# DLRM tower with a three-layer CIN: twelve instead of eleven split groups, another group order, and paced loads for the first chunk

## What is computed

```
e = stack(tbl_f[ids[:, f]] for f in 0..38)        # 512 x 39 x 16
x0 = xk = e
for W, b in ((w0,b0), (w1,b1), (w2,b2)):          # W: 39 x K x 128; K = 39, 64, 64
    z = relu(einsum('bhd,bkd,hks->bsd', x0, xk, W) + b)
    xk, direct part = z[:, :64], z[:, 64:]        # the last layer: all 128 go to direct
logit = sum over d of all direct parts            # 512 x 256
h = relu([logit, dense_ctx] @ W_top1 + b_top1)
h = relu(h @ W_top2 + b_top2)
y = h @ W_top3
```

## Time and profile before

| | us |
|---|---|
| median of 3 runs | 639.19 |
| the runs | 638.8 to 640.38 |
| the profiled execution, its own time | 637.96 |
| its span in the trace | 636.2 |
| PE busy | 604.5 (95%) |
| DVE busy | 552.8 (87%) |
| POOL busy | 459.3 (72%) |
| ACT busy | 304.1 (48%) |

### The profile page before, as it was taken

How to read it: one execution, slowest core, us unless ns; L and a number is a source line. 1 busy time by engine, 2 the same in 40 slices (tenths; PEclk the granted TensorE clock), 3 DMA queues, 4 the chain that set the end, 5 groups by cost and what they waited for, 6 DMA issues and landing times.

```text
span 636.2 us, 7265 instructions
## 1 busy us (share of the span) xinstructions
PE 604.5 (95%) x1934; PEld 364.5 (57%) x1934; DVE 552.8 (87%) x513; ACT 304.1 (48%) x375; POOL 459.3 (72%) x294
## 2 busy tenths in 40 slices
PE   0788899999999999999999999999999999999998
PEld 0334465666666565666666565656666665656653
DVE  1674999999999999999999999999999999999670
ACT  2131654535454555536454645445454646545333
POOL 6638387887878787878878787878878787728350
PEclk9899899999999999999999999999999999999999
DMA  7789887886949495877949495967859494952000
GB/s 254 163 188 222 178 196 163 183 177 143 217 102 217 92 224 119 198 154 160 205 107 218 102 217 112 213 133 180 185 128 220 93 220 99 213 124 79 2 0 0
DMA packets 28703, 98.59 MB, mean 155 GB/s; under 512 B 8113, under 2 KB 17073, under 8 KB 20498
## 3 DMA queue, kind: packets, MB, share of 16 engines
q1 hardware_dynamic: 21832, 93.81, 66.9%
q0 software_dynamic: 5120, 1.32, 2.0%
q10 hardware_dynamic: 1738, 3.33, 1.4%
HBM read 94.60 MB, written 3.84 MB: 155 GB/s over the span
## 4 chain that ended last, share of the span: by engine, by line
PE 89%; DMA 4%; POOL 3%; SPq 2%; issue 1%; ACT 1%; DVE 1%; ACTq 0%
PE z L631 41%; PE z L637 12%; PE z L639 12%; PE z L642 12%; PE z L621 4%; DMA x_rep<-x_rows 3%; POOL gathered L415 3%; PE z L625 2%; PE z L624 2%; PE d_products L718 1%; SPq L319 1%; DMA gathered<-in_tables,rows_sb 1%; PE z L692 1%; SPq L311 0%; DMA base_sb<-in_base 0%
## 5 line engine op out<-in xcount | busy, mean ns | idle before, releaser
L357 POOL TENSOR_TENSOR low<-products,high 128x1024 fp32r<-128x1024 f32 x128 | 303.9, 2389 | 112.4 <-ACT high L759 102.1
L472 DVE TENSOR_TENSOR products<-x_rep,xk 128x1024 f32<-128x1024 f32 (+1 forms) x258 | 333.5, 1339 | 22.3 <-ACT xk L743 13.3
L631 PE MATMUL z<-products,w_whole 128*128 128x512 f32 x640 | 297.8, 596 | 0.1
L759 ACT ACTIVATE high<-products 128x1024 fp32r<-128x1024 f32 x128 | 135.1, 1056 | 133.6 <-DVE products L472 125.1
L637 PE MATMUL z<-high,w_high 128*128 128x512 f32 x352 | 183.7, 522 | 3.1 <-ACT high L759 3.1
L415 POOL DMA_INDIRECT gathered<-in_tables,rows_sb x160 | 153.9, 962 | 44.3 <-issue 41.6
L631 PEld LDWEIGHTS z<-products,w_whole 128*128 128x128 f32 x640 | 121.6, 190 | 104.5 <-issue 93.3
L639 PE MATMUL z<-high,w_low 128*128 128x512 f32 x352 | 138.9, 395 | 0.0
L642 PE MATMUL z<-low,w_high 128*128 128x512 f32 x352 | 109.9, 394 | 1.6 <-POOL low L357 1.3
L637 PEld LDWEIGHTS z<-high,w_high 128*128 128x128 f32 x352 | 66.4, 189 | 41.4 <-issue 25.1
L639 PEld LDWEIGHTS z<-high,w_low 128*128 128x128 f32 x352 | 66.4, 189 | 37.2 <-issue 26.6
(11 more groups left out here) (54 smaller groups left out, 176.2 us busy)
## 6 DMA issues: line engine op xcount, KB each, us to landing
x_rep<-x_rows SPq DMA_DIRECT2D x60, 768.0 KB, 18.8
x_rep<-x_rows SPq DMA_DIRECT2D x64, 512.0 KB, 6.5
x_rows<-gathered SPq DMA_DIRECT2D x16, 225.0 KB
x_rep<-in_w ACTq DMA_DIRECT2D x2, 1280.0 KB, 9.8
gathered<-in_tables,rows_sb POOLq DMA_INDIRECT x160
x_rep<-x_rows SPq DMA_DIRECT2D x4, 384.0 KB, 11.0
x_rep<-x_rows SPq DMA_DIRECT2D x5, 256.0 KB, 6.0
x_same<-x_rows SPq DMA_DIRECT2D x15, 78.0 KB
```

Source lines behind the costliest of these rows:

```text
L357: ops.tensor_tensor(low[0:p, slot, 0:n, :], product(index, p, n), high[0:p, slot, 0:n, :].bitcast(fp32), ALU.subtract).then_inc(low_by[kin ...
L472: nc.vector.tensor_tensor(slots, rep, row.unsqueeze(1).broadcast_to([p, n, N]), ALU.mult).then_inc(made, 1 + pair)
L631: mm = nc.tensor.matmul(out, w_whole[0:p, at, i, :], product(index, p, n)[:, i, :], start=(first and i == 0), stop=(last and i == n - 1))
L759: nc.scalar.activation(high[0:p, slot, 0:n, :], product(index, p, n), ACT.Copy).then_inc(rounded, 1)
```

## The change

- `KINDS`: layer 1 from `wpwpwppwdh` to `wppwdppwdh` (group 2 becomes `p`, 3 becomes `w`, 4 becomes `d`: one split group more), layer 0 from `wsdw` to `sdww`, layer 2 from `wwpwpdpwph` to `wwppwpwpdh` (its `d` is now group 22).
- `LOW_LAG` 2 in place of 1; `GATHERS` two at group 0 and eight at group 14; `logits2` after group 6; ScalarE's `after_layer1` and `after_layer0` one group later.
- First chunk: ten parts of two tiles, and SyncE issues a part only when the part two before it has landed; the second chunk's `write_x0` stands ahead of part 7. `keep_busy(5)` in place of 3 ahead of the selection matmuls; the selector lies in ring slot 7; tile 6 is selected first.

```diff
-FIRST_PARTS = [(4, 6), (0, 4), (6, 8), (8, 10), (10, 14), (14, 17), (17, T1)]
-SELECTED = [0, 1, 6, 2, 3]
+FIRST_PARTS = [(4, 6), (0, 2), (2, 4), *((t, t + 2) for t in range(6, T1, 2))]
+SELECTED = [6, 0, 1, 2, 3]
...
-KINDS = {1: "wpwpwppwdh", 0: "wsdw", 2: "wwpwpdpwph"}
+KINDS = {1: "wppwdppwdh", 0: "sdww", 2: "wwppwpwpdh"}
...
 PAIRED = [0,2]
...
-GATHERS = {1: 1, 6: 9}
+GATHERS = {0: 2, 14: 8}
 assert sum(GATHERS.values()) == GB
-LOW_LAG = 1
-SEL_SLOT = 0
+LOW_LAG = 2
+SEL_SLOT = 7
...
         WRITES = 2
-        WRITTEN_AFTER = 2
+        IN_FLIGHT = 2
+        WRITTEN_WITH = 7
...
             for q in range(1, len(FIRST_PARTS)):
+                if q > IN_FLIGHT:
+                    sp.wait_ge(first_loaded[q - IN_FLIGHT], 32)
+                if q == WRITTEN_WITH:
+                    write_x0(sp, 1)
                 for e in range(2):
                     load_replicated(sp, 0, e, FIRST_PARTS[q], first_loaded[q])
-                if q == WRITTEN_AFTER:
-                    write_x0(sp, 1)
...
-                    if index == 8 and not (isinstance(c, int) and c == 0):
+                    if index == 6 and not (isinstance(c, int) and c == 0):
                         logits2(c - 1)
...
-            keep_busy(3)
+            keep_busy(5)
...
-                    if index == N1 + 3:
+                    if index == N1 + 4:
                         after_layer1(c)
-                    if index == N1 + N0 + 3 and not last:
+                    if index == N1 + N0 + 4 and not last:
                         after_layer0(c)
```

## The result

The changed kernel takes **712.27 us** (median of 4 runs, 710.32 to 712.84), the kernel before in the same session 639.00 us: a ratio of 1.1144, 95% interval 1.1117 to 1.1171. The forecast was 712.0 us. The profiled execution took 710.32 us, the lowest of the four, with a span of 708.5 us against 636.2.

What follows compares the result with a forecast made beforehand. TensorE's matmuls were taken to bound each chunk, with VectorE at 95%. 637.96 + 62.3 + 2.05 + 3.5 = 705.8 us, 707.0 as a median, plus 5 us for the clock gave 712 us; range 688 to 735.

Steps and rivals of the forecast that it cites:

- 1, one split group more: Each chunk: TensorE's own work falls by 0.35 us to 35.13 us; VectorE gets one low part more, GpSimd nothing.
- 2, group 22: Its low part stands behind a double product waiting for TensorE's group 20; TensorE loses 1.7 us a chunk.
- 3, group 2: Its product waits for TensorE's group 23; TensorE waits 2.3 us a chunk, 2.4 with the slower restart.
- 4, VectorE late at group 11: VectorE's low part of group 11 comes late; TensorE waits 0.7 us a chunk, between nothing and 1.2.
- 5, the chunk: A chunk takes 39.9 us for 35.48, 62.3 us over 14 chunks; the last chunk's layer 1 adds 2.05 us.
- 6, the first chunk: New loads gain 1.5 us until tile 6 lands, the new order costs 5.0 behind it: 3.5 us more.
- The clock: Group 2's new waits make the granted clock fall in one chunk in five: 3 x 1.7 = 5 us.
- the two cases seen: Clock in the old trace: half after waits of 2.73 us, or 1.52 and another; full after 1.27 us.
- The rival of unconditional falls: The clock falls in every chunk: 732.5 us; chance 0.12.
- the one with the wait of group 2 alone: Only group 2's wait stays, VectorE being in time at groups 22 and 11: chunk 37.5 us, 672 us; chance 0.10.
- The faster one: The second double product is released early, so the waits at groups 22, 2 and 11 are hidden: 632.4 us; chance 0.04.

Runs made afterwards that it cites:

- e4: The changed kernel with the ring's four empty places spread among the groups instead of all at the chunk's end; 636.98 us, ratio 0.9972.
- g1: f4 with groups 17 and 18 swapped in layer 2 (17 a `w`, 18 a `p`); 632.57 us, ratio 0.9916.
- f4: e4 with layer 0 (`wsdw`) and the selection in the order of the kernel before; 636.11 us, ratio 0.9938.
- e3: The changed kernel with `LOW_LAG` 1 in place of 2; 688.21 us, ratio 1.0760.
- e1: The changed kernel with groups 2 and 3 multiplied one by one instead of in a double product; 685.22 us, ratio 1.0728.
- f2: The kernel before with only the change's new loads of the first chunk; 634.59 us, ratio 0.9931.
- f1: The changed kernel with five extra matmuls put in group 2's wait, between `high` and `low`; 700.98 us, ratio 1.0953.
- g3: The kernel before with three ring places left empty among the groups; 639.34 us, ratio 1.0002.

## Why the prediction was right

Total, direction and mechanism held. Several terms did not, and their errors cancel.

- **1, one split group more:** held. e4 and g1, free of ring waits, take 35.37 and 35.28 us for 35.13. Most of the rest is a low part of GpSimd's that is only just in time (0.23 in f4 at group 17, 0.10 in g1 at group 19, whose pair takes 255.27 - 254.71 = 0.56; in e4 0.10 at group 17, and the other half is VectorE's at group 11). The step "GpSimd keeps its eight low parts, so nothing there" overlooked it: their number is the same, but in layer 2 two of them now stand side by side (16 and 17, in g1 18 and 19).
- **2, group 22:** 1.7 us predicted, 1.66 measured. The idle time of VectorE behind group 20 is 3.5 us; I had said 2.5.
- **3, group 2:** 2.4 us predicted, 2.39 measured, in the two pieces named (`high` 0.66, `low` 1.50; predicted 0.7 and 1.6). e3 and e1 show it to hang on group 23 and on the pair.
- **4, VectorE late at group 11:** 0.7 predicted, 0.46 measured. The low part is there at 225.92, 18.8 us after 207.10, where the sum said 19.2; TensorE would have been there at 18.5, as predicted. e1 shows that its size hangs on the wait of group 2.
- **5, the chunk:** 39.9 predicted, 39.62 measured: 62.3 us predicted for 14 chunks, 58.0 measured. This was 4 us too much. The last chunk's 2.05 us agree with the 2.0 left of the tail's 3.7 when the clock's share is taken off.
- **6, the first chunk:** the term that failed, +3.5 predicted, +0.3 measured. "I take 1.5 us as the net gain": f2 measures it alone as 4.3 us (59.30 for 63.56). The bound that the prediction took, 2.5 us for the dry stretch of the DMA engines, was too low. In the changed kernel, the DMA share from 32 to 35 us is 1.02 instead of 0.15, and the moment came at 59.62, beyond that bound. What else the new loads saved, and whether the pacing or the later write did it, was not taken apart. The second half, what the new order costs behind that moment, was predicted as 29.3 - 24.3 = 5.0 us and is (88.21 - 59.62) - (87.88 - 63.56) = 4.3.

```profile
32.00:35.00 3.00, 1.67 (x6) 0.92 (x6) 1.46 (x2) 0.00 (x0) 1.42 (x2) 1.00 1.02 222
59.62 0.68 DVE L475 TENSOR_TENSOR products<-x_rep,x_bank 64x512 f32<-64x512 f32 x1 [8.03 <-issue]
```

- **The clock:** 5 us predicted, 3 falls at 1.7 us; there were seven in the loop, 10.2 us of time with them, and one in the tail, 1.7. The kernel before has no fall in the tail, and the prediction had no term for one. That the new waits lie between the two cases seen was right; "I take one chunk in five" is what failed, it was one in two, with 1.35 to 1.8 us for each. The Trainium skill (TensorE: Matmul & The Clock Gate, "A second HAM failure mode: psum-queue depth-cycling") says that frequent small idle gaps make the clock oscillate. The trace agrees in part: the clock fell in 7 of 14 chunks with equal gaps, and not in every one. f1 shows that the gap of 1.34 us at group 2 was needed for it; gaps of about that length that stand alone (e1) made no fall in the loop.
- **Sum:** predicted 62.3 + 2.05 + 3.5 + 5 = 72.9 us of span, measured 58.0 + 2.0 + 0.3 + 11.9 = 72.2, for spans that differ by 72.3. Terms 4 to 6 were 7.5 us too large and the clock 6.9 too small. The hit within 0.3 us of the median owes as much to that luck as to the two waits, which were right to 0.1 us; the profiled run that these terms are taken from is besides 2 us under the median, where the prediction allowed 1.2.

The rival of unconditional falls, 732.5 us, and the one with the wait of group 2 alone, 672 us, didn't come. The faster one needed the second pair to be released early. e4 releases both pairs early by the ring's map, and there all the waits in the loop vanish. That the second alone would do, as the rival had it, isn't shown: in e1 the product of group 2 is released early, and group 22 waits as before. The rival's 632.4 us are 4.6 below e4's 636.98; 15 x 0.24 = 3.6 of that are the low parts that are only just in time.

## What to carry to other kernels

When an order of work is changed, redo the ring's look-back: for each group write down whose slot it takes over, and compare the nearest such distance with the group's chain from product to last use (here 6.3 us from the end of group 23 against 4.0 us of work in between). Where places are left over in the last round, spread them; here that gave back 75 us and cost nothing in the kernel that did not need it (g3). An instruction that fills two slots waits for the later of both and delays the earlier, and everything behind it, and a wait that is removed may only uncover the next one, so measure the whole, not the sum.

## Not expected of the hardware

- Chunks whose waits up to the fall agree to 0.03 us (the last one that fell apart) fall to half clock or don't. The falls came at 252.9, 293.9, 334.8 and 375.8 us, and again at 536.2, 577.2 and 618.1: 40.96 us apart, the length of a chunk with a fall to within 0.15 us, with none for three chunks between the two series. The four runs have mean granted clocks of 0.971 to 0.978: the same kernel takes a different number of falls from run to run. What starts or ends a series was not tested.
- A pair of matmuls that has to wait costs 0.57 us to the next start for 0.46, each time; a pair that is just in time costs it too (0.58 in f4 at 254.44, 0.56 in g1 at 254.71), and the trace then shows no wait.
- In the profiled runs of several kernels (e4, f4) the first chunk's selection stood for 3 to 5 us at a time, partly with no releaser shown, and in g1, with f4's code up to there, for 1.2 us at most. In e4 and f4 the granted clock is then 0.50 for 10.2 and 6.8 us, from 31.6 and 36.1 us on. The cause is open. Between the traces of f4 and g1 it makes some 2 us, about as much as the gain that g1 was after.
